# Rows of activations, queries and keys padded to 64 bytes and allocated first, in a Swin block in float32

## What is computed

```
xl = layernorm(x, over the channels);  roll by (-3, -3);  cut into 7 x 7 windows (49 tokens)
q, k, v = qkv(xl)                      # 192 -> 576, 6 heads of 32
attn = softmax(q k^T / sqrt(32));  out = proj(attn v)
xl = layernorm(windows put back, rolled back)
out = x + fc2(gelu(fc1(xl)))           # 192 -> 768 -> 192
```

## Time and profile before

| what | value |
|---|---|
| median of three timed runs | 2942.57 us |
| span of the profiled execution (first to last instruction) | 2938.0 us |
| around the span, by the difference of the two | 4.5 us |
| share of the span in which PE is busy | 98% |
| DVE, ACT, POOL | 90%, 91%, 46% |
| DMA traffic | 213.10 MB, mean 73 GB/s |

### The profile page before, as it was taken

How to read it: one execution, slowest core, us unless ns; L and a number is a source line. 1 busy time by engine, 2 the same in 40 slices (tenths; PEclk the granted TensorE clock), 3 DMA queues, 4 the chain that set the end, 5 groups by cost and what they waited for, 6 DMA issues and landing times.

```text
span 2938.0 us, 74792 instructions
## 1 busy us (share of the span) xinstructions
PE 2892.5 (98%) x26284; PEld 2823.9 (96%) x26284; DVE 2630.3 (90%) x7211; ACT 2686.3 (91%) x5500; POOL 1364.7 (46%) x1549
## 2 busy tenths in 40 slices
PE   5999999999999999999999999999999999999998
PEld 5999999999999999999999999999999999999998
DVE  7899999998999999999999999998999999999985
ACT  3899999999999999999999999999999999999996
POOL 3444444444444444444544444444445444444442
PEclk9999999999999999999999999999999999999999
DMA  5333333323333333333333333333333333333321
GB/s 111 58 77 76 69 73 76 74 68 78 77 69 72 74 78 68 76 78 70 70 73 81 68 72 78 73 68 77 79 68 72 76 77 67 76 74 74 69 62 26
DMA packets 645586, 213.10 MB, mean 73 GB/s; under 512 B 500835, under 2 KB 628580, under 8 KB 645220
## 3 DMA queue, kind: packets, MB, share of 16 engines
q1 hardware_dynamic: 641284, 206.65, 32.3%
q10 hardware_dynamic: 3936, 1.68, 0.3%
HBM read 130.69 MB, written 38.94 MB: 58 GB/s over the span
## 4 chain that ended last, share of the span: by engine, by line
PE 97%; DVE 1%; SPq 1%; ACT 0%; issue 0%; DMA 0%; POOL 0%; POOLq 0%; DVEq 0%; ACTq 0%
PE psum L320 8%; PE psum L321 7%; PE psum L322 7%; PE psum L324 7%; PE psum L323 7%; PE psum L602 7%; PE psum L576 6%; PE psum L556 5%; PE psum L567 5%; PE psum L557 5%; PE psum L568 5%; PE psum L558 5%; PE psum L582 4%; PE psum L330 4%; PE psum L332 3%; PE psum L331 3%
## 5 line engine op out<-in xcount | busy, mean ns | idle before, releaser
L1244 POOL TENSOR_TENSOR pr<-pr,rc 98x294 f32<-98x294 f32 x512 | 385.6, 763 | 378.8 <-DVE rc L1059 378.8
L758 ACT ACTIVATE hh<-psum,b 128x392 fp32r<-128x392 f32 x768 | 451.3, 588 | 47.7 <-PE psum L568 39.0
L761 ACT ACTIVATE hf<-psum,b 128x392 f32<-128x392 f32 x768 | 450.9, 587 | 6.3
L1217 POOL TENSOR_TENSOR ve<-mv,eps 104x4 f32<-104x4 f32 (+1 forms) x256 | 80.6, 315 | 753.5 <-DVE mv L983 753.5
L1238 POOL TENSOR_TENSOR hl<-hf,hh 128x392 fp32r<-128x392 f32 x128 | 226.0, 1766 | 374.4 <-ACT hf L761 374.4
L1046 DVE TENSOR_REDUCE mx<-psum 98x6 f32<-98x294 f32 x512 | 232.5, 454 | 133.3 <-PE psum L577 129.3
L1023 DVE TENSOR_TENSOR hl<-hf,hh 128x392 fp32r<-128x392 f32 x640 | 347.7, 559 | 3.7 <-ACT hf L761 3.7
L320 PE MATMUL psum<-x_h,w_mh 128*128 128x392 f32 x768 | 274.9, 358 | 0.7 <-DVE pr L1051 0.6
L556 PE MATMUL psum<-hh,w2h 128*128 128x392 f32 x768 | 272.9, 355 | 0.0
L715 ACT ACTIVATE pt<-psum 113x294 f32<-113x294 f32 x512 | 206.1, 403 | 70.7 <-PE psum L582 70.4
L576 PE MATMUL psum<-km,qm 128*98 128x98 f32 x2048 | 261.7, 250 | 7.3 <-DVE xn L988 3.4
(11 more groups left out here) (144 smaller groups left out, 10396.6 us busy)
## 6 DMA issues: line engine op xcount, KB each, us to landing
bc<-mean_rstd SPq DMA_DIRECT2D x128, 392.0 KB, 3.6
vbd<-vs SPq DMA_DIRECT2D x512, 73.5 KB
xg<-in_x SPq DMA_DIRECT2D x368, 96.0 KB, 2.5
xt<-in_x SPq DMA_DIRECT2D x112, 194.5 KB, 2.7
out<-xt SPq DMA_DIRECT2D x112, 194.5 KB, 1.9
xt<-in_x SPq DMA_DIRECT2D x112, 97.2 KB, 2.5
out<-xt SPq DMA_DIRECT2D x112, 97.2 KB, 2.1
mean_rstd<-mv SPq DMA_DIRECT2D x384, 1.0 KB
```

The lines of the kernel that those rows point to most:

```text
L758: nc.scalar.activation(hh[:, m % HB, :], bank("fc1", m)[:, 0:T], ACT.Gelu, bias=b1[:, m:m + 1]).then_inc(s_hh, 1)
L761: nc.scalar.activation(hf[:, m % HB, :], bank("fc1", m)[:, 0:T], ACT.Gelu, bias=b1[:, m:m + 1]).then_inc(s_gelu, 1)
```

## The change

Fourteen tensors move to the front of the allocation, behind `ident`: `x1`, `x2`, `o` (three parts each), `o_b`, `hf`, `hh`, `hl`, `qm`, `km`, `qr`, `kr`. Their rows are padded: from 392 to 400 elements (1600 bytes), and from 98 to 112 elements (448 bytes), and views of the first 392 or 98 elements stand for them everywhere else. The five clearings of POOL run over the padded tensors. No instruction is added, removed or moved in any engine's order.

```diff
+ROW = -(-T // 16) * 16
+PAIR_ROW = -(-TP // 16) * 16
 ...
         ident = sb("ident", [128, 128])
+        x1 = [sb(f"x1_{p}", [128, ROW], F32R)[:, 0:T] for p in ("h", "l", "r")]
+        x2 = [sb(f"x2_{p}", [128, ROW], F32R)[:, 0:T] for p in ("h", "l", "r")]
+        o = [sb(f"o_{p}", [128, ROW], F32R)[:, 0:T] for p in ("h", "l", "r")]
+        o_b = sb("o_b", [128, ROW], F32R)[:, 0:T]
+        hf = sb("hf", [128, HB, ROW])[:, :, 0:T]
+        hh = sb("hh", [128, HB, ROW], F32R)[:, :, 0:T]
+        hl = sb("hl", [128, HB, ROW], F32R)[:, :, 0:T]
+        qm_rows = sb("qm", [128, NW, PAIR_ROW])
+        km_rows = sb("km", [128, NW, PAIR_ROW])
+        qr_rows = sb("qr", [128, PAIRS, PAIR_ROW])
+        kr_rows = sb("kr", [128, PAIRS, PAIR_ROW])
+        qm, km, qr, kr = (t[:, :, 0:TP] for t in (qm_rows, km_rows, qr_rows, kr_rows))
         half = sb("half", [128, PAIRS])
 ...
-        x1 = [sb(f"x1_{p}", [128, T], F32R) for p in ("h", "l", "r")]
-        x2 = [sb(f"x2_{p}", [128, T], F32R) for p in ("h", "l", "r")]
-        qm = sb("qm", [128, NW, TP])
-        km = sb("km", [128, NW, TP])
-        qr = sb("qr", [128, PAIRS, TP])
-        kr = sb("kr", [128, PAIRS, TP])
 ...
-        o = [sb(f"o_{p}", [128, T], F32R) for p in ("h", "l", "r")]
-        o_b = sb("o_b", [128, T], F32R)
-        hf = sb("hf", [128, HB, T])
-        hh = sb("hh", [128, HB, T], F32R)
-        hl = sb("hl", [128, HB, T], F32R)
 ...
-            for t in (qm, km, qr, kr, vbd):
+            for t in (qm_rows, km_rows, qr_rows, kr_rows, vbd):
                 nc.gpsimd.memset(t[:], 0.0).then_inc(s_zero_qk, 1)
```

## The result

The changed kernel takes 2936.62 us (median of 13 runs, 2935.72 to 2937.74), the kernel before 2942.74 in the same job (13 runs, 2941.42 to 2944.28): ratio 0.9979, 95% interval 0.9972 to 0.9986. That is 6.1 us, or 0.2%. The forecast was 2939.5, 3.1 us down: the right direction and half the size.

The account below looks back on a forecast made before the run. PE alone was taken as the bound, without gaps. The x1 and x2 starts gave 3.1 us off the 2938.0 span, all else 0: 2934.9, plus 4.5 around it, 2939.4; predicted 2939.5, range 2914 to 2948.

Parts of the forecast that it names:

- PE is the bound and has no gap, so a ns on a matmul is a ns of the run: Whole run: PE alone sets the pace; one ns on each of 75 matmuls a unit is 9.6 us.
- a PE up to 6% faster would still be the bound: Steady part: the other engines have some 44 us in 700 to spare, so PE stays the bound.
- Clearings, ACT and DVE, scores, unchanged starts: POOL's clearings, ACT and DVE work, 24 scores matmuls and 106 matmuls with unchanged starts: each taken to cost 0.
- `x1` and `x2`, 18 odd starts, 3.1 us: Queries, keys and first MLP layer: aligning 18 matmuls saves 1.3 ns each, 24 ns a unit, 3.1 us.
- The difference of differences: Same five matmuls over x1 and x2 with opposite alignments, compared by durations: an odd start costs 1.3 ns.
- `hh` and `hl`, 14 odd starts, 0: Second MLP layer: aligned and odd buffers showed no difference in one trace, so aligning 14 matmuls gains 0.
- Rival B: Alignment pays for all 75 matmuls with 392 columns, which fall to 176 ns: 27 us, 2916; chance 0.20.
- Rival C: New addresses collide in memory; half of the 75 matmuls come to 182 ns: 15 us slower, 2958; chance 0.15.
- Rival D: Aligned stream drops to the rate half the clock shows, apart from a small fixed cost: up to 63 us, 2880; chance 0.03.
- the page: Trainium skill: 165.8 ns for 392 columns; operand start concerns legality, not speed, so the change is worth nothing.
- the half clock: Early 392-column matmuls, 327 ns, read as half clock; half is 163 ns, so 15 to 16 ns each goes elsewhere.

Follow-up runs that it names:

- off8: Changed kernel with only the views moved to element 2, so all 14 tensors start 8 bytes past a multiple of 64: 2957.36 us, ratio 1.0052.
- shift1088: Changed kernel with an unused tensor of 1088 bytes ahead of the 14, all starts modulo 64 kept: 2936.64 us, ratio 0.9981.
- xold: Changed kernel with only x1 and x2 put back to their old starts modulo 64, still in front: 2939.61 us, ratio 0.9998.
- hidold: Changed kernel with only hf, hh and hl put back to their old starts modulo 64, rows unpadded, in front: 2941.49 us, ratio 1.0005.
- o8: Changed kernel with only the three parts of o and o_b at 8 bytes past a multiple of 64: 2938.95 us, ratio 0.9992.
- inplace: Changed kernel's padded tensors declared at their old places instead of in front, all starts 32 modulo 64: 2948.31 us, ratio 1.0022.
- off32: Changed kernel with only the views moved to element 8, so all 14 tensors start 32 bytes past a multiple of 64: 2942.87 us, ratio 1.0003.

## Why the prediction came out half

*PE is the bound and has no gap, so a ns on a matmul is a ns of the run:* right for most of the unit, but not for all of it. The earlier trace rows and their counterparts have PE at 700.00 of 700 in every kernel, and off8 lost time with ACT and DVE less busy than before (633 and 654 of 700), as followers of a slower PE. One thing can't show: since matmuls overlap in the profile, a weight load that is held up for some tens of ns leaves no idle time. It shows at the load for the first hidden tile of `x2`. Before:

```profile
1522.41 0.47 DVE L1051 TENSOR_TENSOR pr<-psum,mx 98x294 f32<-98x294 f32 x1
1522.97 0.25 PE L334 MATMUL psum<-wq_rl,x_r 128*98 128x192 f32 x1
1523.00 0.19 PEld L320 LDWEIGHTS psum<-x_h,w_mh 128*128 128x128 f32 x1
```

After:

```profile
1522.02 0.26 PE L339 MATMUL psum<-wq_rl,x_r 128*98 128x192 f32 x1
1522.02 0.19 PEld L325 LDWEIGHTS psum<-x_h,w_mh 128*128 128x128 f32 x1
```

Before, this load starts 20 ns in the median (2 to 34) after the preceding matmul, after the change 3 or 4 ns. The place waits for DVE (`pr`, the row maximum taken off the last scores): before, the load starts 115 or 116 ns after the end of that instruction in 122 of the 123 units, so it is DVE that lets it go. After the change it is 117 to 126 ns, so PE comes last, by 2 to 11 ns. The matmul there became 23 ns shorter, and the 26 ahead of it together 20 ns longer. shift1088 is like the kernel before in this (115 ns, 16 ns of wait) and its unit is 4 ns from the changed kernel's, so the wait is not what the change gains: PE arrives earlier and waits longer, or later and does not wait. Two things follow. Time won in the 26 matmuls ahead of this place turns into waiting, and nearly all of the net gain, 28 of the 31 ns, lies behind it. And the prediction's sentence that a PE up to 6% faster would still be the bound does not hold here: it took DVE's 44 us of idle time in 700 for slack, where at this hand-over there are some 10 ns a unit. The slack of a hand-over is not the idle time of an engine.

*Clearings, ACT and DVE, scores, unchanged starts:* right as far as they go. `kr` stays at 250 ns in the change, the transposes and `pt` moved by less than 1 ns together. The 40 matmuls with moving weights did change, by up to 8 ns each way and 11 ns in sum a unit (the wrong way), though the prediction had them at 0.

*`x1` and `x2`, 18 odd starts, 3.1 us:* xold says 5.6 us when they alone are put back, 4.2 by its units. In the pair of traces the 18 give 12 ns a unit, 21 at the 12 over `x1` and minus 9 at the 6 over `x2`, where 24 were forecast. The difference of differences rested on each matmul paying for its own start, and the rows after don't bear that out: of the four that lost an odd start only two fell.

*`hh` and `hl`, 14 odd starts, 0:* this is the step that failed, a term put at nothing. The reasoning was that the same instructions over an aligned and an odd buffer take the same time inside one stream, so the start costs nothing. hidold measures 7.6 us (1.0005 against 0.9979, intervals apart), 6.0 by its units. In the change itself the 30 matmuls over `hh` and `hl` became 12 ns a unit faster, 5 at the odd starts and 7 at the aligned ones: more than a third of what the traces have. The comparison was blind because the time need not fall on the odd ones: half of hidold's 47 ns, and the 7 ns of o8 that fell on matmuls that never read `o`, say the same. It was also too coarse: 1.3 ns on each of three matmuls is 4 ns, and starts are printed in steps of 10. The rows were read rightly, but aligned and odd matmuls in one stream are no two samples. That the forecast's direction came out is owed to the mechanism, a cost of the start; that it came within a factor of two is partly luck, since one term was twice too large in the traces and the other missing. Whether the time passes from one matmul to the next, or the pattern is set by when DVE and ACT hand over, the traces do not say: both change together. A third thought, that the weight loads set the pace, the changed kernel does not bear out: in its streams over 392 columns a matmul takes 177.8 ns where the next load has 64 columns (5 places) and 177.9 where it has 128 (58 places).

*Rival B* (alignment at the hand-over, paid in part by the aligned ones) comes nearer to what hidold shows, with the wrong size: 27 us forecast from the best group, 6.1 measured. There is no kernel in which all groups run at 176 ns; one group gets better as another gets worse. In the stream of 25, the five over `x2` from 1509.61 rose from 0.88 to 0.89 us.

*Rival C* (the addresses dealt again) did not carry this change: shift1088 deals them again and stays within 0.6 us. It exists all the same: inplace against off32, equal starts, 5.6 us. Whoever moves a tensor must count with some us either way, here up to 5.6 where aligning all 14 gave 7 to 9.

*Rival D, and the page:* some 14 ns above half of what the half clock shows stay in the aligned kernel too: 4.44 us / 25 = 177.6 ns against 163. The isolated gap of "TensorE: Matmul & The Clock Gate" of the Trainium skill, section "Back-to-back issue gap", comes to an estimate of 165.8 ns for 392 columns. No layout here came near it: the means of this stream lie between 177.3 and 179.6 ns. "SBUF — State Buffer" of the Trainium skill, section "Operand start alignment", calls the start a question of legality and says that speed was not timed; off8 times it: 0.7% of this kernel against the aligned one. The inference drawn from it in the prediction, that the change is worth nothing, is refuted.

What stays open: by what mechanism an odd start slows its own matmul and others, what in the place makes the 5.6 us between off32 and inplace, and whether xold and hidold add up when both are put back in front. The order 0 and 16, then 32, 24, 8 bytes is measured and has no explanation here.

## What to carry to other kernels

Where PE runs full-rate matmuls over 4-byte operands without a gap, give their rows a length and a start that are multiples of 64 bytes; it cost about 2 KB of each partition and brought 0.2 to 0.3% here, and starts at 8 bytes cost 0.7% against it. Don't argue from aligned and odd instructions inside one trace that a start is free, least of all from starts printed in steps of 10 ns: put the views 2, 4 or 8 elements into a padded row, which changes nothing else, and time that. And keep one kernel with everything shifted by a constant beside it, to know how much of a difference of this size is the place. And before calling an engine the only bound, look at when each weight load starts: a wait of tens of ns per unit is in no list of idle times.

## What the runs showed of the hardware

The start costs nothing at half the clock. In off8, in a stretch where the granted clock was 0.50 (54 to 57 us), the matmuls with 392 columns are 0.32 to 0.33 us apart:

```profile
55.62 0.53 PE L326 MATMUL psum<-x_h,wq_ml 128*128 128x392 f32 x1
55.94 0.53 PE L327 MATMUL psum<-x_l,wq_mh 128*128 128x392 f32 x1
56.27 0.53 PE L328 MATMUL psum<-x_r,wq_rh 128*128 128x392 f32 x1
```

In ns it is 326 and 327, as in the kernels before and changed. The stretch of the earlier trace rows and of the prediction, at 42 us, has the same distance, but the profile holds no record of the clock that early and prints 1.00. In off8 the first record is a rise to 1.00 at 43.66 us, and the distance falls from 326 to 187 ns at 43.67; so half the clock was the right reading.

And with float32 operands, which pass more slowly (85 to 87 ns from one start to the next for 98 columns, so about 2.1 clocks a column at 2.4 GHz), it costs nothing at the full clock: `kr` of off8, at 8 modulo 64, where that of the changed kernel is at 0 (the 24 matmuls over `km` and `kr` together take 4 ns a unit more, all of it at the first two behind the stream over `hh`):

```profile
L582 PE MATMUL psum<-kr,qr x992: 250/250/250, 103.4 to 2879.8; 128*98 128x98 f32 x199
```

Only the faster stream of float32r columns (177.6 ns for 392, so 1.1 clocks a column) was seen to be sensitive. Within one trace its pace is a pattern and not chance: at one place in the unit it repeats within 1 ns in nearly all of the 123 like units (at 184 of the 205 places before, 197 after, all 205 in off32 and off8), while the distances over the unit, inside the streams of 392 columns, spread between 172 and 188 ns before the change. That the pattern is the same in every execution of a kernel is not shown, since each has one trace.
